# The last attention turn of a fused decoder layer written out with its own order

## The reference

```python
# attention (HGRN): all projections with ternary weights and 8-bit activations
i = silu(bitlinear(x, Wi)) * (1 - f);  f = sigmoid(bitlinear(x, Wf))
h = scan over tokens: h = f * h + i
o = rmsnorm(bitlinear(x, Wg)) * g_norm_weight * (h * sigmoid(h))
x = layernorm(x + bitlinear(o, Wo))
# experts: token id picks one of 4 matrices of ctx (gate, up and down are the same matrix)
x = layernorm(x + (silu(x @ C.T) * (x @ C.T)) @ C)
# mix: eight 512 x 512 factors
x = layernorm(x + (sum over r of x @ factor[r]) / sqrt(8) + bias)
```

## Time and profile before

| | before |
|---|---|
| time, median of 3 runs | 372.42 us (371.88 to 375.5) |
| the profiled execution | 369.25 us, its span in the trace 367.5 us |
| PE busy | 285.9 us (78%) |
| DVE, ACT, POOL busy | 225.3, 230.8, 200.5 us (61%, 63%, 55%) |
| TensorE clock, mean | 0.92 of full |

### The profile page before, as it was taken

The page is one execution under the profiler, slowest core; times in us unless marked ns, Lnnn a source line. Parts: engine busy times, 40 slices in busy tenths (PEclk is TensorE's granted clock), DMA queues, the critical chain, the costliest instruction groups (busy, mean ns, idle before and its releaser), DMA issues.

```text
span 367.5 us, 5728 instructions
## 1 busy us (share of the span) xinstructions
PE 285.9 (78%) x1506; PEld 215.5 (59%) x1518; DVE 225.3 (61%) x488; ACT 230.8 (63%) x456; POOL 200.5 (55%) x381
## 2 busy tenths in 40 slices
PE   1376467575687997998998895999399999999960
PEld 1254235242575675676876674777288888888640
DVE  4799999999387579839656753452234444444420
ACT  4779877977367696777777666256145555555441
POOL 2455867858546348466565837546044444444542
PEclk9998859695599999999999999899799999999996
DMA  8999968753883530003012101201401111100000
GB/s 261 389 387 374 228 117 160 143 138 89 198 162 62 94 115 2 29 40 105 0 48 75 54 29 77 69 29 42 131 29 57 52 38 59 57 30 24 28 7 0
DMA packets 17406, 37.02 MB, mean 101 GB/s; under 512 B 1503, under 2 KB 1631, under 8 KB 17376
## 3 DMA queue, kind: packets, MB, share of 16 engines
q0 software_dynamic: 6496, 15.74, 18.6%
q1 hardware_dynamic: 10880, 20.92, 17.2%
HBM read 26.68 MB, written 10.76 MB: 102 GB/s over the span
## 4 chain that ended last, share of the span: by engine, by line
PE 36%; POOL 6%; issue 6%; DMA 5%; ACT 4%; DVE 3%; POOLq 0%; ACTq 0%; DVEq 0%; SPq 0%
PE bank_m L1264 4%; PE bank_m L1268 4%; PE bank_m L1265 4%; PE bank_z L1264 3%; PE bank_z L1265 3%; DMA sorted_rows<-r,place 3%; PE bank_z L1268 3%; PE bank_y L1264 3%; PE bank_y L1265 3%; PE bank_y L1268 3%; DMA rows<-sorted_rows 2%; POOL n_d L313 2%; PE bank_tr L1235 2%; PE bank_q L1235 2%; POOL x L353 1%
## 5 line engine op out<-in xcount | busy, mean ns | idle before, releaser
L312 POOL TENSOR_SCALAR n_v<-n_dev 128x1 f32<-128x1 f32 (+1 forms) x46 | 10.1, 220 | 60.9 <-ACT x L626 28.5
L1264 PE MATMUL bank_y<-c_hi,h_hi 128*128 x76 | 32.2, 424 | 3.1 <-ACT h_hi L594 1.5
L1264 PE MATMUL bank_z<-c_hi,a_hi 128*128 x76 | 32.8, 432 | 1.9 <-ACT a_hi L594 1.9
L1264 PE MATMUL bank_m<-f_hi,m_hi 128*128 128x512 f32 x76 | 31.6, 416 | 3.4 <-DVE f_lo L876 2.6
L895 DVE TENSOR_TENSOR act_z<-bank_z,act_z 128x512 f32<-128x512 f32 x19 | 13.1, 691 | 34.3 <-ACT act_z L608 34.3
L358 POOL DMA_INDIRECT out<-r,token_of x19 | 20.6, 1087 | 23.1 <-ACT r L633 19.9
L1265 PE MATMUL bank_z<-c_lo,a_hi 128*128 x76 | 31.7, 417 | 0.0
L1265 PE MATMUL bank_y<-c_lo,h_hi 128*128 x76 | 30.8, 405 | 0.0
L313 POOL TENSOR_TENSOR n_d<-n_v,minus_half 128x1 f32<-128x1 f32 (+1 forms) x46 | 28.3, 615 | 3.8
L1265 PE MATMUL bank_m<-f_lo,m_hi 128*128 128x512 f32 x76 | 30.1, 396 | 0.0
L353 POOL TENSOR_TENSOR x<-x,bias_b 128x512 f32<-128x512 f32 x19 | 25.0, 1315 | 9.0 <-PE bank_q L1235 8.8
(11 more groups left out here) (205 smaller groups left out, 855.6 us busy)
## 6 DMA issues: line engine op xcount, KB each, us to landing
f_sum<-in_factors POOLq DMA_DIRECT2D x7, 1024.0 KB, 10.6
rows<-sorted_rows SPq DMA_DIRECT2D x19, 256.5 KB, 2.9
xs<-in_x SPq DMA_DIRECT2D x8, 512.0 KB, 6.2
c_stage<-in_ctx_t SPq DMA_DIRECT2D x4, 1024.0 KB, 14.3
sorted_rows<-pad_row SPq DMA_DIRECT2D x1, 1539.0 KB, 20.6
w_stage<-in_wf_t SPq DMA_DIRECT2D x1, 1024.0 KB, 8.4
w_stage<-in_wi_t SPq DMA_DIRECT2D x1, 1024.0 KB, 10.6
w_stage<-in_wg_t SPq DMA_DIRECT2D x1, 1024.0 KB, 12.8
```

The costliest lines, as they stand in the source:

```text
L1264: t.matmul(bank[:], hi[:, c, :], w_hi(c), start=(c == 0), stop=False)
```

## The change

The loops now stop before turn 8, and turn 8 stands behind them in an order of its own on PE, ACT, DVE and POOL (SP is as before). Besides, `low_of_factors` stands ahead of `residual_2` and `low_a` in turn 5, and `mix(0)` waits for one chunk of f_lo at a time. The core of the diff:

```diff
@@ POOL
+                p, n = N_GROUPS - 1, TAIL - 2
+                scale_o(p)
+                quantise_o(p)
+                power_3(n - 3)
+                token_of_row(n)
+                power_2(n - 1)
+                add_bias(n - 2)
+                store(n - 3)
+                number_rows(p)
+                power_1(p)
+                scatter_rows(p)
+                power_3(n - 2)
+                token_of_row(n + 1)
+                add_bias(n - 1)
+                store(n - 2)
+                power_2(n)
@@ ACT
+                p, n = N_GROUPS - 1, TAIL - 2
+                silu_z(n - 1)
+                square_o(p, 0)
+                square_o(p, 1)
+                high_h(n - 1)
+                square_3(n - 3)
+                high_a(n)
+                norm_3(n - 3)
+                square_2(n - 1)
+                o_by_channel(p)
+                high_m(n - 2)
+                norm_2(n - 1)
+                silu_z(n)
+                square_1(p)
+                high_h(n)
+                square_3(n - 2)
+                norm_1(p)
+                high_a(n + 1)
+                norm_3(n - 2)
+                high_m(n - 1)
+                square_2(n)
+                norm_2(n)
@@ DVE
+                    if turn == MERGE + 2:
+                        low_of_factors()
                     residual_2(n - 1)
                     low_a(n)
-                    if turn == MERGE + 2:
-                        low_of_factors()
...
+                p, n = N_GROUPS - 1, TAIL - 2
+                output(p, 0)
+                hidden(n - 1)
+                output(p, 1)
+                max_o(p, 0)
+                max_o(p, 1)
+                low_h(n - 1)
+                residual_3(n - 3)
+                low_a(n)
+                residual_2(n - 1)
+                low_m(n - 2)
+                hidden(n)
+                residual_1(p)
+                low_h(n)
+                residual_3(n - 2)
+                low_a(n + 1)
+                residual_2(n)
+                low_m(n - 1)
@@ PE
+                        if s_split is not None:
+                            pe.wait_ge(s_split, c + 1)
...
+                p, n = N_GROUPS - 1, TAIL - 2
+                silu_h_by_token(p)
+                mix(n - 3)
+                transpose_h(n - 1)
+                down(n - 1)
+                transpose_a(n)
+                after(pe, s.tml, n - 2)
+                transpose_o(p)
+                pe.wait_ge(s.oqt, p + 1)
+                transpose_m(n - 2)
+                up(n)
+                project_back(p)
+                mix(n - 2)
+                transpose_h(n)
+                transpose_a(n + 1)
+                down(n)
+                transpose_m(n - 1)
+                up(n + 1)
```

More of the change, by code:

```diff
@@ L449, in _ @@
                 add_factor(6)
-                for turn in range(MERGE + 1, N_GROUPS + 1):
+                for turn in range(MERGE + 1, N_GROUPS):
                     g, p, n = turn, turn - 1, 2 * turn - LEAD
@@ L458, in _ @@
                     token_of_row(n)
-                    if is_group(g):
-                        scale_g(g)
+                    scale_g(g)
                     if n >= 2:
@@ L706, in _ @@
                     high_h(n - 1)
[L707 to L713, removed]
+                    tanh_f(g, 0)
+                    tanh_f(g, 1)
+                    silu_i(g, 0)
+                    silu_i(g, 1)
+                    forget(g, 0)
+                    forget(g, 1)
                     high_a(n)
                     square_2(n - 1)
-                    if is_group(g):
-                        square_g(g, 0)
-                        square_g(g, 1)
+                    square_g(g, 0)
+                    square_g(g, 1)
                     if is_group(g + 1):
@@ L722, in _ @@
                     norm_2(n - 1)
-                    if is_group(g):
-                        silu_h(g, 0)
+                    silu_h(g, 0)
                     if n >= 2:
                         high_m(n - 2)
-                    if is_group(g):
-                        silu_h(g, 1)
+                    silu_h(g, 1)
                     if n >= 3:
@@ L1056, in _ @@
                     output(p, 1)
-                    if is_group(g):
-                        rescale_f(g, 0)
-                        rescale_f(g, 1)
+                    rescale_f(g, 0)
+                    rescale_f(g, 1)
                     low_h(n - 1)
-                    if is_group(g):
-                        rescale_i(g, 0)
-                        rescale_i(g, 1)
+                    rescale_i(g, 0)
+                    rescale_i(g, 1)
                     max_o(p, 0)
@@ L1068, in _ @@
                         quantise_x(g + 1)
+                    if turn == MERGE + 2:
+                        low_of_factors()
                     residual_2(n - 1)
                     low_a(n)
-                    if turn == MERGE + 2:
-                        low_of_factors()
[L1073 to L1077, removed]
+                    gate_i(g, 0)
+                    scans(g, 0)
+                    gate_i(g, 1)
+                    scans(g, 1)
                     if n >= 3:
@@ L1081, in _ @@
                         low_m(n - 2)
-                    if is_group(g):
-                        weigh_g(g, 0)
-                        weigh_g(g, 1)
+                    weigh_g(g, 0)
+                    weigh_g(g, 1)
                     hidden(n)
@@ L1259, in transpose_m, with product @@
                     rows_by_channel(bank_q, x2[:, n % RING, :], s.tm)
-                def product(n, bank, hi, lo, w_hi, w_lo, s_hi, s_lo, s_done):
+                def product(n, bank, hi, lo, w_hi, w_lo, s_hi, s_lo, s_done, s_split=None):
                     pe.wait_ge(s_hi, n + 1)
                     for c in range(KC):
+                        if s_split is not None:
+                            pe.wait_ge(s_split, c + 1)
                         t.matmul(bank[:], hi[:, c, :], w_hi(c), start=(c == 0), stop=False)
@@ L1289, in mix @@
                     after(pe, s.r3, n)
-                    if n == 0:
-                        pe.wait_ge(s.fsplit, KC)
-                    product(n, bank_m, m_hi, m_lo, lambda c: f_hi[:, c, :], lambda c: f_lo[:, c, :], s.tmh, s.tml, s.m)
+                    product(n, bank_m, m_hi, m_lo, lambda c: f_hi[:, c, :], lambda c: f_lo[:, c, :], s.tmh, s.tml, s.m,
+                            s.fsplit if n == 0 else None)
                 ranks_in_tiles()
@@ L1328, in _ @@
                 up(0)
-                for turn in range(MERGE + 1, N_GROUPS + 1):
+                for turn in range(MERGE + 1, N_GROUPS):
                     g, p, n = turn, turn - 1, 2 * turn - LEAD
                     silu_h_by_token(p)
-                    if is_group(g):
-                        project_f(g)
+                    project_f(g)
                     transpose_h(n - 1)
-                    if is_group(g):
-                        project_i(g)
+                    project_i(g)
                     if n == 1:
@@ L1341, in _ @@
                     transpose_a(n)
-                    if is_group(g):
-                        project_g(g)
+                    project_g(g)
                     if is_group(g + 1):
```

## The result

| | before | changed |
|---|---|---|
| time, median of 8 runs each | 372.87 us (371.83 to 375.5) | 367.38 us (365.52 to 370.26) |
| ratio, 95% interval | | 0.9852 (0.9818 to 0.9887) |
| profiled execution, its span | 369.25 us, 367.5 us | 365.52 us, 363.7 us |
| TensorE clock, mean over the span | 0.92 | 0.928 |

Compared again on two other occasions, the same kernel gave 0.990 (0.986 to 0.994) and 0.982 (0.976 to 0.988): 3.6 and 5.0 us by medians.

What follows compares the result with a forecast made beforehand. PE bounds the kernel from 272 us, so the end follows up(11)'s start (264.94) and clock. Turn 5 -0.6 and turn 8 +0.5 give -0.1; kept clock at up(11) -1.5: -1.6, 370.8 us, range 368.2 to 373.4.

Steps and rivals of the forecast that it cites:

- Turn 5: Factors ahead of residual_2(2): of mix(0)'s 2.6 us wait only 0.6 is gained, transpose_m(1) then waiting for xq_t.
- mix(6) moved up: Turn 8: fills the 2.78 us wait, so down(8) should keep full clock; transpose_a(9) still waits for rows, gaining nothing.
- The new wait: Turn 8, PE ahead of transpose_m(7): 3.7 us idle for ACT's oq_t, behind square_2(8) and residual_2(8).
- POOL's arm ends last: Before up(11): scatter, store(7), power_2(9), norm_2(9), then hidden(10) set its start, 263.7 or 265.4, instead of slot 11's rows.
- my sum: Turn 8 to the start of up(11), without turn 5: -1.2 us with clock kept, +0.5 with clock low.
- 1.5 us at up(11): Half clock until 268.0 after the 5.5 us wait costs 1.5 us; a kept clock there was taken as likelier.
- 1.7 lost again at up(9): After turn 8's new wait, half speed for about the first 3.4 us of work: +1.7 us.
- The factors bring 2.6: Rival, turn 5: the whole 2.6 us is gained because x_by_channel(6) doesn't end the wait; 368.8 us, chance 0.05.
- kept in turn 8: Rival: the clock stays full after turn 8's 3.7 us wait; -3.3 us, 369.1 us, chance 0.14.
- POOL's arm makes it slower: Rival: indirect DMAs and a longer half clock delay POOL's arm, and the clock falls again; +1.6 us, 374.0, chance 0.14.
- the two that the prediction rested on: PE stretches that ended in half clock: 0.66 us of work in 4.7 us around 228, 5.5 us idle around 260.

Runs made afterwards that it cites:

- 20 fillers: Kernel before plus 20 matmuls that nothing reads, between transpose_h(10) and the transposes of slot 11's rows: ratio 0.999 (0.995 to 1.002).
- old order, all filled: Kernel before plus unread matmuls in three PE waits: 9 ahead of mix(0), 11 ahead of transpose_h(8), 26 ahead of slot 11's rows: 369.17 us against 372.79.
- new order, filled: Changed kernel plus 14 matmuls that nothing reads, between transpose_o(7) and the wait for oq_t: ratio 0.9845 (0.980 to 0.989) against the kernel before.

## Why the prediction was wrong

The last-turn stretch in all traces that bear on the sum:

| turn 8 | traces, us | mean |
|---|---|---|
| old order | 45.14, 46.49, 45.82, 46.40 (20 fillers), 46.83 | 46.14 |
| old order, all filled | 43.17 | |
| new order | 42.74, 44.23, 44.10, 44.26, 43.42 | 43.75 |
| new order, filled | 42.13 | |

- **Turn 5: -0.6 forecast, -0.65 in the traces.** Right, with its mechanism: the wait moved from f_lo to xq_t, 145.10 for a forecast 145.1. That the clock times agree to 0.1 us is partly luck, since the changed kernel's down(2) began 0.45 us later than before (134.36 against 133.91).
- **mix(6) moved up, worth nothing by itself.** Right in place: down(8) kept its clock, and transpose_a(9) waits 0.81 us for the rows. Worth nothing held for the first trace alone, where the half clock under down(8) ended about as slot 9's rows landed; in three of the four others slot 9's transposes came 0.4 to 0.8 us later still.
- **The new wait, 3.7 us forecast, 3.52 measured** in every trace, from ACT's oq_t, as said. Moving o_by_channel cut it to 1.16, which shows the cause.
- **POOL's arm ends last.** Right: PE no longer waits for slot 11's rows, transposes of slot 10 wait for act_z, and with power_2(9) moved ahead (and the ACT steps with it) 1 us of the stretch goes, 39.88 to 38.93. Even its size was near: with the clock kept, the forecast has 39.6 us from the silu transposes to up(11) (263.7 - 224.1), and the filled kernel's trace has 39.2 (267.01 - 227.78).
- **The order of turn 8 alone**, both filled, is worth 43.17 - 42.13 = 1.0 us; my sum has 1.2 for the kept clock, counted from a trace with half clock in it: up to the start of up(11) the filled old order takes 40.28 us (266.17 - 225.89), the first trace 40.85. Nearly all of that 0.57 is the transposes of slot 11's rows at half clock: they begin after 38.96 us there and after 38.91 in the filled order.
- **The step that failed is the price of half clock, on the side of the kernel before.** It entered the sum as 1.5 us at up(11), with nothing for down(8), against 1.7 lost again at up(9), so that the two about cancelled. In five traces of the old order half clock and what follows from it cost on average 46.14 - 43.17 = 3.0 us in the last-turn stretch, and 2.0 in the first; in the new order 43.75 - 42.13 = 1.6 us. Each filled order is one trace. Of the 3.0, 1.8 stand at up(11) (4.29, 5.20, 4.33, 4.44, 5.28 against 2.88), 0.4 between the transposes of slot 11's rows and up(11), and 0.7 ahead of them (they begin after 39.62 us on average, 38.91 filled), where down(8)'s half clock comes in; in two of the five the wait for slot 11's rows is also longer (6.07 and 5.83 against 5.51 us), which isn't shown to be the clock's doing. The sum over the traces is thus 0.65 + 1.0 + 1.4 = 3.1 us and not 1.6.
- **How it came about.** The first trace of the new order is 1.0 us quicker than its mean too, so the first pair of traces differs by 2.40 us in the stretch, as the means do (2.39). It is the forecast that set unlike executions side by side. For the new order it has 41.3 us to up(11) (265.4 - 224.1) and 2.9 for it, 44.2 together, which is what three of the five new traces took; from that it subtracted the old trace with the shortest stretch, 45.14 for a mean of 46.14. The prediction says itself that this execution lay 3.2 us under the median, and applied the difference to the median without asking what the slower executions consist of. That is 1.0 of the missing 1.5 us; the other 0.4 to 0.5 is that the new order took 43.75 us on average and not 44.2.
- **From 3.1 to the 3.6 to 5.5 us of the timed runs** (3.7 to 6.8 by the ratios). What is left isn't shown. The timed runs of the old order that the ratios count have a mean clock of 0.908 (67 runs), the five profiled executions 0.914; with the new turn 8 it is 0.922 in both. In each of the four series of the kernel before, a mean clock lower by 0.01 goes along with 0.8 to 1.5 us, weakly, which would make 0.5 to 0.9 us of the difference. That is a correlation. The filled old kernel gains 3.6 us timed, where the traces have 3.0 in the stretch, but with an interval of 2.4 to 4.9. The rest stays open.
- **The rivals.** "The factors bring 2.6" (368.8) and "kept in turn 8" (369.1) are nearest in time, but neither is what happened: transpose_m(1) is released by xq_t, and up(9) runs at 0.68 and 0.52 in the first two traces. "POOL's arm makes it slower" named the arm, not the size. No rival let the kernel before cost more than its one trace.

## What to carry to other kernels

The same order with the same waits can cost nothing at one place or 1.5 to 2.4 us of half clock, from one execution to the next. Price the clock by several traces, and for both sides of the comparison by executions of the same kind: an average forecast subtracted from a quick trace is too small by that trace's luck. Fill a wait with matmuls that nothing reads to measure what its clock costs; fill it to the end, since with 1.5 us left over up(11) lost as much as without fillers. When an order is rewritten, look on each in-order engine for what the awaited instruction stands behind: one line moved on ACT brought another 3.9 us of the last-turn stretch.

## What the runs showed of the hardware

- The clock went to half level after waits much shorter than the two that the prediction rested on: after 1.48 us, transposes and 0.78 us (with 4.8 us of dense matmuls ahead of it), after 2.75 us in one execution while 2.59 and 2.69 us left it whole in two others, and after 1.48 and 1.16 us while 1.11 and 1.16 did not.
- Ahead of the last product, mix(18), PE waits 1.13 to 1.15 us, does a set of transposes and waits 0.78 us in all 16 traces. In nine the product ran at the full clock, in seven at half for most of it: 1.5 us. The same program point with the same waits differs from one execution to the next.
- A half clock, once there, lasted from about 3 us (236.79 to 239.8 in the changed kernel's first trace) to about 7 us (228.76 to 235.7 with turn 5 alone changed). up(11) lost 1.4 to 2.4 us by it in five executions with the old turn 8.
- 26 matmuls that nothing reads, 6.2 us of PE's time where it otherwise waited 5.5 to 6.1 us, made the kernel faster by 2.8 us of the median, by 1.6 to 4.2 us by the ratio's interval.
